# A second output on Vector's one-hot comparisons in a four-layer graph network

## The reference, cut to what matters

```
h = relu(layernorm(x));  x = x + L0(h)   # mean over edges of h[src] * weight, then two products
h = relu(layernorm(x));  x = x + L1(h)   # attention with a softmax over each target's edges
h = relu(layernorm(x));  x = x + L2(h)   # products of h[src] and edge_attr, batch norm, silu, mean over edges
h = relu(layernorm(x));  x = x + L3(h)   # segment_sum(h[src], dst)
```

## Time and profile before

| | us |
|---|---|
| median of 3 runs | 2232.41 |
| lowest and highest | 2232.05, 2232.51 |
| the profiled execution, its own time | 2232.63 |
| its span in the trace | 2230.9 |
| mean granted clock of TensorE, share of full | 0.742 |

### The profile page before, as it was taken

One profiled execution on the slowest core, in us unless ns is written; L12 is line 12 of the kernel. 1 busy time (PEld: TensorE's weight loads), 2 busy tenths in 40 slices (PEclk: granted clock), 3 DMA queues, 4 the chain that ended last, 5 costly groups with the idle time before them and its releaser, 6 DMA issues. The chain is left out here.

```text
span 2230.9 us, 22598 instructions
## 1 busy us (share of the span) xinstructions
PE 1422.8 (64%) x6447; PEld 1112.4 (50%) x6447; DVE 1432.5 (64%) x2200; ACT 778.1 (35%) x1056; POOL 1491.4 (67%) x1468
## 2 busy tenths in 40 slices
PE   2778777786444444444340598999956258787871
PEld 1555555554434334334340476777733147676760
DVE  6777777777647767777774654665576465665652
ACT  1333333333134434343330344444455123333420
POOL 5777777776457777777765477777601267777864
PEclk9866667666666555666655699999955579998995
DMA  5222222222145444444442343444254023333321
GB/s 131 80 83 80 81 74 78 83 79 75 40 119 161 147 145 160 148 160 151 150 143 76 74 92 76 96 95 87 61 169 158 19 58 80 85 83 82 91 62 47
DMA packets 214865, 220.82 MB, mean 99 GB/s; under 512 B 107694, under 2 KB 167555, under 8 KB 214531
## 3 DMA queue, kind: packets, MB, share of 16 engines
q1 hardware_dynamic: 163971, 143.64, 21.3%
q0 software_dynamic: 47072, 62.55, 12.9%
q10 hardware_dynamic: 3744, 13.63, 1.6%
HBM read 118.24 MB, written 101.46 MB: 98 GB/s over the span
## 5 line engine op out<-in xcount | busy, mean ns | idle before, releaser
L600 POOL DMA_INDIRECT gathered<-table,idx x1336 | 1374.4, 1029 | 535.8 <-issue 411.4
L1665 DVE COPY_PREDICATED spare<-spare,psum 64x512 f32<-64x512 uint8 x246 | 181.3, 737 | 200.1 <-ACT spare L1203 194.1
L897 PE MATMUL psum<-rounded 128*128 128x512 f32 x1092 | 278.7, 414 | 23.2 <-DVE rounded L1657 23.2
L897 PEld LDWEIGHTS psum<-rounded 128*128 128x128 f32 x1092 | 216.9, 202 | 69.2 <-issue 23.6
L859 PE MATMUL psum<-ident,arena 128*128 128x128 f32 x208 | 57.9, 434 | 290.6 <-ACT arena L1145 290.6
L634 POOL DMA_INDIRECT arena<-scan,rowidx x100 | 103.2, 1032 | 174.2 <-DMA scan<-ea 106.7
L859 PEld LDWEIGHTS psum<-ident,arena 128*128 128x128 f32 x208 | 37.2, 217 | 306.1 <-issue 170.1
L1203 ACT ACTIVATE spare<-psum 64x512 f32<-64x512 f32 x82 | 48.3, 589 | 375.7 <-PE psum L897 375.2
L1048 ACT ACTIVATE arena<-psum 128x1024 f32<-128x1024 f32 x52 | 53.2, 1024 | 239.0 <-PE psum L724 147.3
L1156 ACT ACTIVATE arena<-arena 128x1024 f32<-128x1024 f32 x52 | 54.9, 1056 | 226.1 <-DVE arena L1584 226.1
L897 PE MATMUL psum<-rounded_keep 128*128 128x512 f32 x480 | 130.2, 421 | 0.0
(11 more groups left out here) (253 smaller groups left out, 3165.1 us busy)
## 6 DMA issues: line engine op xcount, KB each, us to landing
scan<-arena SPq DMA_DIRECT2D x52, 768.0 KB, 3.6
scan<-ostage SPq DMA_DIRECT2D x130, 256.0 KB, 2.2
gathered<-table,idx POOLq DMA_INDIRECT x1336, 2.6
d_mlp<-arena ACTq DMA_DIRECT2D x26, 512.0 KB, 2.7
arena<-d_mlp SPq DMA_DIRECT2D x52, 256.0 KB, 2.7
ea<-in_edge_attr SPq DMA_DIRECT2D x104, 128.0 KB
spare<-src_row SPq DMA_DIRECT2D x82, 128.0 KB, 3.2
spare<-src_quarter SPq DMA_DIRECT2D x82, 96.0 KB, 2.9
```

The costliest lines, as they stand in the source:

```text
L600: pool.indirect_dma_start(out=out[:, j, hf, :], out_offset=None, in_=tab[layer], in_offset=bass.IndirectOffsetOnAxis(ap=idx[:, j, hf * NCH ...
L897: last = nc.tensor.matmul(P[:, bank + t, :], parts[layer][n][:, b:b + 2, :].rearrange("p b d -> p (b d)"), tile(layer, m, u)[:, hf * CH:(h ...
L1665: picked = v.copy_predicated(rows[m % 2][halves[hf], :], quarter[m % 2][halves[hf], q - 1, :], P[halves[q % 2], bank + q // 2, :])
```

## The change

The comparison in `make_onehots` gets a second operation, `ALU.add`, and a second output: the sum along each row, one number per partition, written to `small[:, 6, u]`. Nothing reads it. The one-hot tile itself is as before. All 205 one-hot comparisons of Vector have this form afterwards, 100 in layer 2 and 105 in layer 3. No instruction changes its place in a queue.

```diff
                     if n_used(layer, m, u):
                         dve.wait_ge(S(f"L{layer} onehots used"), n_used(layer, m, u))
-                    v.tensor_scalar(tile(layer, m, u), rowb[m % 2], rowcol[:, 0, u:u + 1], None, ALU.is_equal) \
+                    v.tensor_scalar(tile(layer, m, u), rowb[m % 2], rowcol[:, 0, u:u + 1], None, ALU.is_equal, ALU.add,
+                                    accum_out=small[:, 6, u:u + 1]) \
                         .then_inc(S(f"L{layer} DVE onehots made"), 1)
```

## The result

| | before | after |
|---|---|---|
| median of the runs on one chip, us | 2232.46 | 2161.61 (2161.45 to 2162.31) |
| ratio | | 0.9682, 95% interval 0.9665 to 0.9699 |
| span of the profiled execution, us | 2230.9 | 2160.6 |

The prediction was 2161 us. A second output that nobody reads took 71 us off, 3.2%, although Vector has 107 us more to do.

The account below looks back on a forecast made before the run. No engine is busy over 67%; GpSimd's gathers, held by one-hots, were taken to pace layer 3, and TensorE layer 2. 59.7 + 12.3 = 72.0 us less than 2232.63 gave 2160.6, rounded to 2161; range 2152 to 2190.

Parts of the forecast that it names:

- GpSimd sets the pace of layer 3, and one-hots hold it: Layer 3: gathers pace it; one meeting four one-hots took 3.51 us instead of 0.94 or 0.95; excess 61.9 us.
- The slot of the new one-hot: Vector, start to start: 1.22 to 1.51 us, taken as 1.35, where it was 0.68 before.
- 59.7 us of GpSimd in layer 3: Layer 3 gathers: the 61.9 us excess goes, less some 0.7 for casts and about 1.5 for scatter.
- 2.2 was allowed for: Layer 3 gather excess expected to stay: some 0.7 us from two casts and about 1.5 us of small scatter.
- Two signs named in the prediction: Layer 3 gathers: longest near 1.1 us outside the first two; L600 near 236 us busy.
- TensorE and Vector keep up: Layer 3, per five chunks: Vector 28.8 us and TensorE 27.5 fit within GpSimd's 29.9, so GpSimd stays the bound.
- Layer 2, 12.3 us: Layer 2 net gain: 11.9 us of gather waits plus 4.1 of clock, less 3.7 for one-hot u = 4.
- the clock instead of 4.1: Layer 2, TensorE after two waits: 2.5 and 1.6 us lost to the lower clock, 4.1 together, won back.
- GpSimd staying held: Rival, chance 0.09: new form still holds gathers; beside four one-hots about 6.2 us, total 2340; if fast plus sum write, 2247.
- Vector as the bound: Rival, chance 0.15: longer one-hots make Vector pace layer 3; 2178 us at a 1.6 us slot, even with GpSimd at 1.46.

Follow-up runs that it names:

- one-layer kernels: Two kernels against the one before: second output in layer 3 alone, 2173.35 us (0.9750); in layer 2 alone, 2218.52 us (0.9948).
- the kernel with two inputs: Kernel before with each one-hot a tensor_tensor comparison of two SBUF inputs, no sum: 2308.33 us, 1.0354.
- the kernel with the plain pair: Changed kernel with layer 2's one-hots u = 4 and 6 plain again: 2155.51 us, 0.9663 to before.

## Why the prediction was right, point by point

**GpSimd sets the pace of layer 3, and one-hots hold it.** Right, shown by the one-layer kernels and by the gathers: 296.01 us of them became 241.05 with the plain form gone, and the layer 55.0 us shorter.

**The slot of the new one-hot, 1.35 us between 1.22 and 1.51.** The rate was right (1.266 us against 1.22 to 1.27). The read of the sum takes 0.08 us and lies wholly beside a comparison that follows, so that neighbours are 1.20 us apart. Over the five of a chunk, those ahead of a pick or a running sum included, the slot is (4.92 + 1.29) / 5 = 1.24 us: inside the range, at its low end. Vector's sum per five chunks is 27.8 us, where 28.8 was worked out, and the reserve is the larger for it.

**59.7 us of GpSimd in layer 3.** It was 55.0, and this is the term that was mis-sized. The step behind it said that every Vector instruction at the slow rate lets gathers pass. One kind does not: the running sum of a multiplied chunk reads two inputs from SBUF (`keep` and `spare`), and a gather that begins in it, but for its very start, is held until it ends and for 0.75 us more. Timeline of the changed kernel, Vector and then GpSimd (1961.07 + 1.28 = 1962.35, and 1961.56 + 1.55 = 1963.11):

```profile
1961.07 1.28 DVE L1769 TENSOR_TENSOR_SCAN scan_ring<-keep,scan_ring,spare 128x512 f32<-128x512 uint8 x1
```
```profile
1961.56 1.55 POOL L600 DMA_INDIRECT gathered<-table,idx  x1 [0.30 <-issue]
```

It comes once in nearly every period (the period is 30.55 us, 24 gathers without it 29.94), eleven times in all, and makes 6.2 us. The excess left in layer 3 is 241.05 - 248 x 0.944 = 6.9 us, where 2.2 was allowed for: the 4.7 us by which the term is off. The rest of the excess that I had put on single one-hots was partly this hold. Two signs named in the prediction missed for the same reason: the longest gather is 1.85 us and not near 1.1, and the gathers stand at 241 us and not near 236.

The trace of the kernel before had the counterexample already. The running sum that the prediction looked at, at 1957.26, is that of a fetched chunk, with its second input in PSUM. In layer 1 a running sum reads both from SBUF, and the gather that began 0.09 us after its start took 1.93 us, again until 0.75 us after its end, with no one-hot near. Vector, then GpSimd:

```profile
819.14 1.27 DVE L1580 TENSOR_TENSOR_SCAN arena<-arena 128x512 f32<-128x512 f32 x1
```
```profile
819.23 1.93 POOL L600 DMA_INDIRECT gathered<-table,idx  x1 [0.30 <-issue]
```

**TensorE and Vector keep up.** Right, and thinner than stated for TensorE. Vector's sum came out at 27.8 us instead of 28.8, but TensorE's 27.5 us was too low: its own period is 29.0 us, with a wait of 0.99 us for the running sum in it that was not in the sum. GpSimd's 30.55 hides both: TensorE waits 1.35 us per period for gathers, and GpSimd waited for a buffer 1.8 us in all.

**Layer 2, 12.3 us.** TensorE's stretch there, from its first transposes (1258.88, now 1259.83) to the first product for the batch norm behind it (1623.86, now 1611.55), is 13.3 us shorter. The waits for gathers, 11.9 us, are all gone. TensorE waits 0.57 us for u = 4 eight times, 4.6 us where it was 0.8: 3.8 us against 3.7 predicted. That leaves 13.3 + 3.8 - 11.9 = 5.2 us for the clock instead of 4.1. TensorE's busy time over the stretch agrees: 346.3 us before and 341.3 after, 5.0 less for the same 1608 products and transposes. The kernel before, then the changed one:

```profile
1258.80:1623.80 365.00, 346.30 (x1608) 0.98 0.39 86
```
```profile
1259.80:1611.50 351.70, 341.31 (x1608) 0.99 0.41 89
```

**What was not in the sum.** 1.9 us more went on either side of TensorE's stretch of layer 2, 1.0 of them in a late-row gather (L634) behind it that took 1.97 us before and 0.94 now, and 1.3 us behind the last gather; 1.2 us came on top ahead of layer 2. All three lie outside the changed code, and nothing here tells them from the scatter between executions. So the total (70.3 us of span against 72.0) is nearer than its parts: layer 3 was taken 4.7 us too well and the rest some 3 us too badly. That the forecast of 2161 met 2161.61 so closely is luck; the mechanism and the size of the main term are not.

**The rivals.** GpSimd staying held did not happen with the sum, but the kernel with two inputs is that rival in the flesh: 2308 us against 2340 worked out for it, and 5.65 us for the gather beside four one-hots against 6.2. Vector as the bound needed 0.28 us more per one-hot than the change gave.

## What to carry to other kernels

Before an instruction is made cheaper, look at what the engine beside it does meanwhile: Vector's time per instruction was the wrong price here, the time of the gather beside it the right one. A form that takes 70% longer but leaves GpSimd alone can make the faster kernel, as long as its own engine has that much idle time per period; add up the slots of one period to see whether it has. Work moved off the pacing engine pays where the engine that takes it over is waiting at that moment, and comes back as lag where it is not.

## What the runs showed of the hardware that I had not expected

- Reading out the sum takes 0.07 to 0.09 us in all 205 cases. In front of a comparison or a statistics instruction (144 of them) it costs no slot: that instruction starts with it, in all but one. In front of a pick or a running sum (61) the next one starts at least 0.10 us after it. Part of that is there without the sum as well: a plain one-hot ahead of a running sum has a slot of 0.76 us instead of 0.68.
- An instruction of Vector at the slow rate with two inputs in SBUF holds a gather as a fast one does: 5.65 us beside four comparisons of 1.21 us, and up to 1.85 us beside one running sum. The same running sum with its second input in PSUM leaves it at 0.94.
- How long plain one-hots hold a gather goes by what stands ahead of them more than by when they begin. In the kernel before, a gather that began less than 0.95 us ahead of two or four one-hots right behind a pick was held to the end of the last one in 33 cases of 34. Where back-to-back one-hots stood behind anything else it was never held beyond the first (9 cases, and 19 in the kernel with the plain pair). Two examples are a pair behind a pick, below, that began 0.14 us into a gather and held it for 2.36 us (kernel before, GpSimd, then Vector), and the pair behind a statistics instruction, above, that began 0.23 us into one and made it 1.09 us long:

```profile
1436.92 2.36 POOL L600 DMA_INDIRECT gathered<-table,idx  x1 [0.30 <-issue]
```
```profile
1437.06 1.39 DVE L1657 TENSOR_SCALAR rounded_keep<-spare,rowcol 128x1024 fp32r<-128x1024 uint16 x2
```

- A gather held to the last one-hot behind a pick ended 0.82 us after it where the one-hots began up to 0.38 us into the gather, and 0.12 us after it where they began 0.49 us or more into it. So a held gather has one of two amounts of its 0.94 us left. What it needs at these two points, and why the pick matters, stays open; no run was made for it.
